# Fused LoRA-routed layer on one core: h transposed by transfers and VectorE instead of TensorE, a ring of four, tile 0 ordered by operand

## What is computed

```
logits = x @ Wr.T + 5.0 * one_hot(id, 8)
gates  = softmax of the two largest logits, scattered to their two experts, else 0
h      = (x @ A[e].T) for 8 experts of rank 16, each times its gate   (128 values per token)
cond   = x @ W.T + 2.0 * sum over experts of h[e] @ B[e].T
out    = x + softplus(scale) * (cond @ sign)
```

## Time and profile before

| | before |
|---|---|
| median of 3 runs, us | 165.47 (165.2 to 165.47) |
| the profiled execution's own time, us | 165.39 |
| its span, us | 163.6 |
| TensorE busy | 97% |
| VectorE, ScalarE, GpSimd busy | 59%, 40%, 32% |
| DMA, mean over the span | 119 GB/s |
| x loads, y stores: from issue to landing, us | 1.8, 2.1 |

### The profile page before, as it was taken

How to read it: one execution, slowest core, us unless ns; L and a number is a source line. 1 busy time by engine, 2 the same in 40 slices (tenths; PEclk the granted TensorE clock), 3 DMA queues, 4 the chain that set the end, 5 groups by cost and what they waited for, 6 DMA issues and landing times.

```text
span 163.6 us, 3711 instructions
## 1 busy us (share of the span) xinstructions
PE 159.1 (97%) x1070; PEld 154.3 (94%) x1070; DVE 96.5 (59%) x416; ACT 66.1 (40%) x177; POOL 51.7 (32%) x50
## 2 busy tenths in 40 slices
PE   7999989999999999999999999999999999999993
PEld 5788779999999999999999999999999999999992
DVE  5668995565566655555555555566655555455741
ACT  3653642434443333444443433443333444443340
POOL 2984435222223333333333222223333333333000
PEclk9999999999999999999999999999999999999999
...
GB/s 190 355 145 133 110 47 118 75 117 117 123 123 113 127 118 124 128 128 128 128 124 99 102 118 119 116 123 120 120 115 127 128 128 128 64 64 64 68 66 128
DMA packets 29431, 19.51 MB, mean 119 GB/s; under 512 B 7248, under 2 KB 24432, under 8 KB 29424
## 3 DMA queue, kind: packets, MB, share of 16 engines
...
HBM read 11.03 MB, written 8.39 MB: 119 GB/s over the span
## 4 chain that ended last, share of the span: by engine, by line
PE 94%; DVE 4%; ACT 1%; issue 0%
PE pair L643 69%; PE pair L663 14%; PE p_b L581 2%; PE p_ht L670 2%; PE pair L593 2%; PE pair L600 2%; PE pair L607 2%; DVE wide_lo L489 1%; DVE m_full L483 1%; PE pair L575 0%; PE pair L573 0%; PE pair L574 0%; ACT wide_hi L372 0%; DVE xt L435 0%; DVE wide_lo L475 0%; ACT y L398 0%
## 5 line engine op out<-in xcount | busy, mean ns | idle before, releaser
L300 POOL TENSOR_TENSOR xt_lo<-xt,xt_hi 128x512 fp32r<-128x512 f32 x32 | 41.2, 1288 | 91.1 <-ACT xt_hi L350 91.1
L643 PE MATMUL pair<-wide_hi,xt_hi 128*128 128x392 f32 (+1 forms) x256 | 63.0, 322 | 0.7 <-DVE wide_lo L489 0.6
L643 PE MATMUL pair<-wide_lo,xt_hi 128*128 128x392 f32 (+1 forms) x256 | 60.1, 311 | 0.0
L643 PE MATMUL pair<-wide_hi,xt_lo 128*128 128x392 f32 (+1 forms) x256 | 60.1, 311 | 0.0
L643 PEld LDWEIGHTS pair<-wide_hi,xt_hi 128*128 128x128 f32 x256 | 39.5, 189 | 1.6 <-DVE wide_lo L489 0.9
L643 PEld LDWEIGHTS pair<-wide_hi,xt_lo 128*128 128x128 f32 x256 | 39.8, 188 | 0.0
L643 PEld LDWEIGHTS pair<-wide_lo,xt_hi 128*128 128x128 f32 x256 | 39.8, 188 | 0.0
L397 ACT ACTIVATE y<-pair 128x256 f32<-128x256 f32 x31 | 11.9, 384 | 44.3 <-PE pair L663 44.3
L520 DVE TENSOR_TENSOR logits<-pair,bias 128x8 f32<-128x8 f32 x32 | 5.3, 166 | 37.0 <-PE pair L643 37.0
L435 DVE STREAM_TRANSPOSE xt<-x_in 128x512 f32<-128x512 f32 x32 | 22.7, 710 | 3.7 <-DVE top L528 3.2
L350 ACT ACTIVATE xt_hi<-xt 128x512 fp32r<-128x512 f32 x32 | 20.3, 633 | 2.1 <-DVE xt L435 2.1
...
## 6 DMA issues: line engine op xcount, KB each, us to landing
x_in<-in_x SPq DMA_DIRECT2D x128, 64.0 KB, 1.8
out<-y SPq DMA_DIRECT2D x31, 256.0 KB, 2.1
sign_in<-in_L_ffn_sign ACTq DMA_DIRECT2D x4, 256.0 KB, 5.2
w_in<-in_L_cond_W SPq DMA_DIRECT2D x4, 256.0 KB, 4.9
a_in<-in_L_cond_A SPq DMA_DIRECT2D x4, 64.0 KB, 5.1
b_in<-in_L_cond_B SPq DMA_DIRECT2D x4, 64.0 KB, 4.0
...
```

What stands on the lines that cost most here:

```text
L300: nc.gpsimd.tensor_tensor(xt_lo[n][:, :, :].rearrange("p j (g b) -> p g j b", g=NQ), xt[n][:, :, :, :], xt_hi[n][:, :, :].bitcast(FP32).re ...
L643: last = nc.tensor.matmul(pair[n][bank][:, at0:at0 + hi - lo], l[:, k, :], w[:, k, lo:hi], start=(opens and k == 0 and l is xt_hi[n] and w ...
```

## The change

- All rings have four buffers (RING), and LAG is three: `lora` in step s is for tile s - 3. The PSUM pairs take all eight banks; p_b2 is bank 0 of pair 3 (tile 3 waits for b2's low part), and p_ht is gone from the loop.
- h of tiles 0 to 28: SP issues four transfers from h_gated to h_moved (`move_h`), each of 32 columns from 128 partitions to 32 partitions in four rows, 128 bytes a piece. VectorE transposes h_moved in 32x32 blocks to ht in SBUF (`turn_h` on VectorE, right behind the logits), ScalarE makes ht_hi from it (`high_h`) and VectorE ht_lo, behind the maximum and ahead of x's transposition. ht_hi and ht_lo are written with a stride of four elements.
- h of tiles 29 to 31 is still transposed by TensorE (`turn_h(tile)` in `finish`), into banks of pairs that are free by then.
- Loads of x from tile 4 on: two of the four transfers are issued by SP, one tile of the ring ahead, and two by ScalarE (`load`), behind its xt_hi.
- `finish` is reordered: it now holds five groups of `lora`.
- Tile 0 (`first_tile`): all chunks of high-high first, then xt_lo times high, then high times wide_lo. b2's products with B's high part come first, then those with its low part.
- Written out in the prologue (not shown): ScalarE makes b_hi after the head's high parts, and xt_hi of tile 1 after all of M's high parts, with the four load issues for tiles 4 and 5 ahead of b2's high part. VectorE's order is fold 0, low parts of the head, b_lo, folds 1 to 3, transposition of x of tile 1, low parts of M's chunks 0, 2, 3 (before: b_lo, head, folds 0 and 1, transposition, low 0, folds 2 and 3, low 2 and 3). GpSimd makes xt_lo of tile 0 ahead of the bias.

The diff, without lines in which only S3 became RING and without the prologue's moved lines:

```diff
...
-h_gated = sb("h_gated", [P, ER])
+h_gated = [sb(f"h_gated{n}", [P, ER]) for n in range(RING)]
+h_moved = [sb(f"h_moved{n}", [P, NQ, Q]) for n in range(RING)]
+ht = sb("ht", [ER, NQ, Q])
...
 pair = [[ctx.enter_context(nc.psum_tensor(f"pair{n}{k}", [P, 512], FP32)) for k in range(2)]
-        for n in range(S3)]
-p_ht = ctx.enter_context(nc.psum_tensor("p_ht", [P, 512], FP32))
-p_b2 = ctx.enter_context(nc.psum_tensor("p_b2", [P, 512], FP32))
+        for n in range(RING)]
+p_b2 = pair[3][0]
 p_m = [pair[1][0], pair[1][1], pair[2][0], pair[2][1]]
+p_ht = {TILES - 3: pair[(TILES - 1) % RING][1], TILES - 2: pair[(TILES - 4) % RING][0],
+        TILES - 1: pair[(TILES - 4) % RING][1]}
...
+    return q + (r + d) // RING
 LEAD = 2
-LAG = 2
-FIRST = LAG + S3
...
+    def move_h(q, r, d):
+        n = slot(r, d)
+        sp_eng.wait_ge(h_gated_made, RING * q + r + d + 1)
+        for i in range(NQ):
+            sp_eng.dma_start(h_moved[n][Q * i:Q * i + Q, :, :], h_gated[n][:, Q * i:Q * i + Q])\
+                .then_inc(h_arrived[n], 16)
     def turnover(q, r, s):
-        if s is None or s + S3 < TILES:
-            sp_eng.wait_ge(xt_made, S3 * q + r + 1)
-            load(q, r, S3 * q + r + S3)
+        if s is None or 0 <= s - LEAD - 1 < LATE:
+            move_h(q, r, -LEAD - 1)
+        if s is None or s + RING < TILES:
+            sp_eng.wait_ge(xt_made, RING * q + r + 1)
...
+    def load(q, r, d):
+        n = slot(r, d)
+        act.wait_ge(xt_made, RING * q + r + d + 1 - RING)
+        for i in range(NQ // 2, NQ):
+            act.dma_start(x_in[n][Q * i:Q * i + Q, :, :], x_load[i, :, RING * q + r + d, :, :])\
+                .then_inc(x_loaded[n], 16)
+    high_x(0, 1, 0, first=True)
+    load(1, 0, 0)
+    load(1, 1, 0)
...
+    def high_h(done, late):
+        if late is None:
+            act.wait_ge(ht_made, done - LAG + 1)
+            nc.scalar.activation(ht_hi[:, :].rearrange("p (b g) -> p g b", g=NQ), ht[:, :, :], ACT.Copy)\
+                .then_inc(ht_hi_made, 1)
+        else:
+            act.wait_ge(ht_turned, late - LATE + 1)
+            act.wait_ge(y_summed, late)
+            nc.scalar.activation(ht_hi[:, :], p_ht[late][:, 0:P], ACT.Copy).then_inc(ht_hi_made, 1)
     def step(q, r, s):
-        if has(s, -LAG):
-            act.wait_ge(ht_turned, S3 * q + r - LAG + 1)
-            nc.scalar.activation(ht_hi[:, :], p_ht[:, 0:P], ACT.Copy).then_inc(ht_hi_made, 1)
+        if s is None or 0 <= s - LAG < LATE:
+            high_h(RING * q + r, None)
...
+        if s in (TILES - 1, TILES, TILES + 1):
+            high_h(s, s - 2)
...
         if has(s, LEAD):
-            high_x(q, r, LEAD, first=(s is not None and s + LEAD < S3))
+            high_x(q, r, LEAD, first=(s is not None and s + LEAD < RING))
+        if has(s, LEAD + RING):
+            load(q, r, LEAD + RING)
...
-    def low_h(done):
-        dve.wait_ge(ht_hi_made, done - LAG + 1)
-        nc.vector.tensor_tensor(ht_lo[:, :], p_ht[:, 0:P], ht_hi[:, :].bitcast(FP32), ALU.subtract)\
-            .then_inc(ht_lo_made, 1)
+    def low_h(done, late):
+        dve.wait_ge(ht_hi_made, done - LAG + 1 if late is None else late + 1)
+        if late is None:
+            nc.vector.tensor_tensor(ht_lo[:, :].rearrange("p (b g) -> p g b", g=NQ), ht[:, :, :],
+                                    ht_hi[:, :].bitcast(FP32).rearrange("p (b g) -> p g b", g=NQ),
+                                    ALU.subtract).then_inc(ht_lo_made, 1)
+        else:
+            nc.vector.tensor_tensor(ht_lo[:, :], p_ht[late][:, 0:P], ht_hi[:, :].bitcast(FP32),
+                                    ALU.subtract).then_inc(ht_lo_made, 1)
+    def turn_h(q, r, s):
+        n = slot(r, -LAG)
+        dve.wait_ge(h_arrived[n], 16 * NQ * (turn(q, r, -LAG) + 1))
+        nc.vector.transpose(ht[:, :, :].rearrange("p g b -> p (g b)"),
+                            h_moved[n][:, :, :].rearrange("p g c -> p (g c)")).then_inc(ht_made, 1)
     def step(q, r, s):
-        done = S3 * q + r
+        done = RING * q + r
         n = slot(r, -1)
         if has(s, -1):
...
                 .then_inc(logits_made, 1)
             dve.wait_ge(logits_made, done)
-        hurry = s is not None and s >= TILES - 1
-        if has(s, -LAG) and not hurry:
-            low_h(done)
+        if s is None or 0 <= s - LAG < LATE:
+            turn_h(q, r, s)
+        if s == TILES:
+            low_h(done, TILES - 3)
         if has(s, -1):
             nc.vector.max(top[:, :], logits[:, :]).then_inc(top_made, 1)
+        if s is None or 0 <= s - LAG < LATE:
+            low_h(done, None)
+        if has(s, -1):
             dve.wait_ge(top_made, done)
         if s == 0:
             turn_x(q, r, LEAD, first=True)
             low_b2()
         elif has(s, LEAD):
-            turn_x(q, r, LEAD, first=(s is not None and s + LEAD < S3))
+            turn_x(q, r, LEAD, first=(s is not None and s + LEAD < RING))
         if has(s, -1):
             nc.vector.max_index(top_at[:, :], top[:, :], logits[:, :]).then_inc(top_at_made, 1)
-        if has(s, -LAG) and hurry:
-            low_h(done)
         if has(s, -1):
             dve.wait_ge(top_at_made, done)
             nc.vector.tensor_copy(top_no[:, :], top_at[:, 0:2]).then_inc(top_no_made, 1)
...
+        if s == TILES + 1:
+            low_h(done, TILES - 1)
...
+    pe.wait_ge(b_hi_made, 1)
+    for j in range(OC):
+        for part in (sign_hi, sign_lo):
+            nc.tensor.matmul(p_b2[:, :], b_hi[:, j, :, :].rearrange("p e r -> p (e r)"), part[:, j, :],
+                             start=(j == 0 and part is sign_hi), stop=False, skip_group_check=True)
     pe.wait_ge(b_lo_made, 1)
     for j in range(OC):
-        last = three(p_b2[:, :], b_hi[:, j, :, :].rearrange("p e r -> p (e r)"),
-                     b_lo[:, j, :, :].rearrange("p e r -> p (e r)"),
-                     sign_hi[:, j, :], sign_lo[:, j, :], j == 0, j == OC - 1)
+        last = nc.tensor.matmul(p_b2[:, :], b_lo[:, j, :, :].rearrange("p e r -> p (e r)"), sign_hi[:, j, :],
+                                start=False, stop=(j == OC - 1), skip_group_check=True)
...
+    def first_tile():
+        for l, w in ((xt_hi[0], wide_hi), (xt_lo[0], wide_hi), (xt_hi[0], wide_lo)):
+            if w is wide_hi and l is xt_hi[0]:
+                pe.wait_ge(head_hi_made, 2)
+            elif w is wide_hi:
+                pe.wait_ge(xt_lo_made, 1)
             else:
-                pe.wait_ge(m_lo_made, (1, 0, 2, 3)[k])
+                pe.wait_ge(head_lo_made, 1)
+            for k in range(KC):
+                if w is wide_hi and l is xt_hi[0]:
+                    pe.wait_ge(m_hi_made, k + 1)
+                elif w is wide_lo and k == 1:
+                    pe.wait_ge(m_lo_second_made, 1)
+                elif w is wide_lo:
+                    pe.wait_ge(m_lo_made, (1, 0, 2, 3)[k])
+                for bank, lo, hi in BANKS:
+                    last = nc.tensor.matmul(pair[0][bank][:, 0:hi - lo], l[:, k, :], w[:, k, lo:hi],
+                                            start=(k == 0 and w is wide_hi and l is xt_hi[0]), stop=False,
+                                            skip_group_check=True)
+                    if w is wide_lo and k == KC - 1:
+                        last.then_inc((head_ready, wide_done)[bank], 1)
     def lora(n, banks):
...
-        pe.wait_ge(h_gated_made, done)
-        nc.tensor.transpose(p_ht[:, 0:P], h_gated[:, :], ident[:, :]).then_inc(ht_turned, 1)
+    def turn_h(tile):
+        pe.wait_ge(h_gated_made, tile + 1)
+        nc.tensor.transpose(p_ht[tile][:, 0:P], h_gated[tile % RING][:, :], ident[:, :]).then_inc(ht_turned, 1)
     def step(q, r, s):
-        done = S3 * q + r
-        if has(s, 0):
+        done = RING * q + r
+        if s == 0:
+            first_tile()
+        elif has(s, 0):
             pe.wait_ge(xt_lo_made, done + 1)
-            if s is None or s >= S3:
-                pe.wait_ge(y_copied, done - S3 + 1)
-            for k in range(KC // 2):
-                m_there(s, k)
-                wide(r, [k], BANKS, opens=True)
+            if s is None or s >= RING:
+                pe.wait_ge(y_copied, done - RING + 1)
+            if s == RING - 1:
+                pe.wait_ge(b2_lo_made, 1)
+            wide(r, range(KC // 2), BANKS, opens=True)
         if has(s, -LAG):
-            if s == LAG:
-                pe.wait_ge(b2_lo_made, 1)
             pe.wait_ge(ht_lo_made, done - LAG + 1)
             lora(slot(r, -LAG), (0, 1)).then_inc(y_summed, 1)
-        if has(s, 0):
-            for k in range(KC // 2, KC):
-                m_there(s, k)
-                wide(r, [k], BANKS, signals=True)
-        if has(s, -1):
-            turn_h(done)
+        if s != 0 and has(s, 0):
+            wide(r, range(KC // 2, KC), BANKS, signals=True)
     def finish(s):
-        before, r, n = (s - 1) % S3, s % S3, s % S3
+        before, r = (s - 1) % RING, s % RING
         first, second = range(KC // 2), range(KC // 2, KC)
```

(94 more changed lines are left out.)

80 lines of the change are left out of this document (37 added, 43 removed).

## The result

| | before | after |
|---|---|---|
| median, us | 165.33 (165.2 to 165.47, 4 runs) | 169.46 (167.77 to 169.75, 4 runs) |
| profiled execution, us | 165.39 | 169.75 |
| its span, us | 163.6 | 167.6 |
| chain that ended last | TensorE 94% | SyncE's queue 49%, TensorE 19% |

The ratio is 1.0215, 95% interval 1.0177 to 1.0254. The forecast was 162.1, faster by 2%: the wrong side.

A forecast was written before the change was run, and what follows sets the result against it. TensorE, without gaps in the loop, was taken as the bound. From 165.39, -3.19 (transposition), -1.34 (prologue) and +1.14 (finish) gave 162.0, forecast 162.1 with the median's 0.08; own range 161.5 to 162.8, full range 161.1 to 164.3.

The forecast's parts named there:

- SyncE's sum in part 2: Loop, SyncE's queue: four moves, two x loads and the store take 3.2 of a 4.27 us step, so in time.
- may be late by more than a step: Loop, SyncE: loads four tiles ahead and a store buffer needed four tiles later leave room for lateness.
- (a): Rival, loop: ScalarE's load issues delay the h matmuls; at 0.8 an issue 6.8 us more, 168.8; chance 0.09.
- (d): Rival, loop: moves land late and VectorE waits for h; 3.2 us lost again, 165.2; chance 0.05.
- the 0.10 given to "slower": Whole kernel: chance 0.10 of a slower result, made of (a) and a part of (d).
- The sign of being wrong: Loop: TensorE idle each step released by ht_lo, with ScalarE issues over 0.6 or VectorE waiting on h_arrived.
- b_in's 1.13 an issue: Upper bound for ScalarE's load issues, from four b_in issues taking 4.51; the likely value was 0.47 each.
- Tile 1 at 23.99, not 22.6: Prologue: tile 0 by operand removes gaps, -1.34 us, so tile 1 starts at about 22.6.
- 0.3 of slack: Loop's start: tile 0's moved h has two short steps of 3.56 ahead and about 0.3 us of slack.
- My own sentence on the exclusion of VectorE and GpSimd: Prologue: VectorE instructions with two SBUF inputs and GpSimd ones reading SBUF exclude each other; without it 0.2 us less.
- The forecast gaps of 0.49, 0.1, 0.3 and 0.25: Finish: TensorE waits before heads of tiles 31 and 28 and for h of tiles 30 and 31; together +1.14 us.
- The transposition's price: Loop: taking h's transposition off TensorE saves 0.11 in each of 29 tiles, -3.19 us; step 4.38 becomes 4.27.

The follow-up runs named there:

- run 5: The changed kernel with SyncE issuing one of each tile's four x loads and ScalarE three: 164.32 us, ratio 0.9916 to the kernel before.
- run 6: The changed kernel with SyncE issuing three of each tile's four x loads and ScalarE one: 180.0 us (one run).
- run 1: The changed kernel with no x load on SyncE in the loop, ScalarE issuing all four from tile 6 on: 164.55 us, ratio 0.9941 to before.
- run 2: The kernel before with only the change's prologue, transposition still on TensorE and lag two: 164.99 us, ratio 0.9976.
- run 7: The kernel before with four transfers of the move's shape added to each SyncE loop step, read by nobody: 188.58 us (one run).
- run 9 on the kernel before: run 2 with GpSimd waiting in step 1 for VectorE's gate of tile 0: 163.88 us, ratio 0.9894 to the kernel before.
- run 8: run 5 with own buffers for h parts of tiles 29 to 31, tile 31's transposition ahead of tile 30's h matmuls: 163.54 us, ratio 0.9883 to before.
- run 9 on run 8: run 8 with GpSimd waiting in step 1 for VectorE's gate of tile 0: 163.68 us, ratio 0.9881 to the kernel before.

## Why the prediction was wrong

**The step that failed** is SyncE's sum in part 2: "4 x 0.46 + 2 x 0.46 + 0.4 for the store, 3.2 of 4.27". It measured 4.46. Two terms were wrong. The move was priced by the x load's 0.46 from one issue to the next, and takes 0.60 with 0.04 behind it: four take 2.5, not 1.84, +0.66. And between the groups, where the waits and the address registers stand, 0.5 to 0.9 a step passes, 0.66 on the mean, which the sum put at nothing. The timeline of SyncE before shows such times already (0.36 and 0.18 here between the loads' end and the store, with no wait for y in this stretch), and I did not ask for it:

```profile
60.27 1.85 SPq L227 DMA_DIRECT2D x_in<-in_x  x4
62.48 0.37 SPq L233 DMA_DIRECT2D out<-y  x1
64.82 1.82 SPq L227 DMA_DIRECT2D x_in<-in_x  x4
66.82 0.37 SPq L233 DMA_DIRECT2D out<-y  x1
```

Either term alone would have left the sum at 3.8; with both the queue was over 4.27, and no slack in time ("may be late by more than a step") helps against a queue that is over the step in sum. No rival had SyncE: (a) put the danger on ScalarE, (d) on the landing, so the 0.10 given to "slower" stood on causes that did not come. The sign of being wrong did come, VectorE waiting for the moves and TensorE released by ht_lo, but I had meant it for late landings; the moves landed in 1.8 and were issued late. The part had a row for the landing's upper end and none for the issue's, though b_in's 1.13 an issue stood in it and was used for ScalarE alone. Four moves at that price would have been 4.5.

The Trainium skill, in "DMA: Bandwidth & Descriptors", section "Issuing engines are not separate DMA queues", says that issuing on several engines only saves the time on the sequencer, "which is usually small relative to the DMA itself". The first half agrees with runs 5 and 6: moving an issue changes the time only through SyncE's sequence, and the landings of moves, loads and stores stay at 1.9 to 2.2. The second half doesn't hold here: 0.60 to issue beside 1.8 to land, and with seven issues a tile the issue time was the kernel's bound.

**The sum, against the profiled execution.** Forecast 162.0, measured 169.75.
- Tile 1 at 23.99, not 22.6: +1.4. The order by operand works (one gap, 0.45, where I had 0.2), but W and sign landed late in this execution: ScalarE waited 1.82 for a part of W, and TensorE 1.32 for b_hi, which the change had put behind the head's parts. In runs 1 and 2 tile 1 started at 22.23 and 22.28, in run 5 at 23.00. Whether the new order makes a late W dearer wasn't tried.
- Tile 0's h parts: TensorE waits 0.94 for them, +0.9. I had 0.3 of slack; the gate of 1.29 took it. My own sentence on the exclusion of VectorE and GpSimd covered the low parts, not the gate.
- The steady steps, 26 from the first group of h matmuls at 33.86 to the one at 149.88: 26 x (4.46 - 4.27) = +5.0.
- The finish, from tile 30's first load to the end of the last: 12.27, I had 12.26, 0. The forecast gaps of 0.49, 0.1, 0.3 and 0.25 measured 0.60, 0, 0.25 and 0.19.
- From the last weight load to the end of the run 5.1, before 4.76: +0.35. It lies around the span: after and the six kernels built on it have 2.07 to 2.25 there, before and the four built on it 1.76 to 1.86, run 7 with its idle moves among them. So it isn't the moves' traffic; its cause is open.

Together +7.65, of 7.75.

**What held.** The transposition's price, in part: the step without SyncE's bound is 4.30, not 4.27; its 0.11 gave 0.08 back, -2.3 in place of -3.2. ScalarE's issues run beside its activations, as two issues of after at 71.48 and 71.97 do:

```profile
71.39 0.38 ACT L432 ACTIVATE y<-pair 128x256 f32<-128x256 f32 x1
71.48 0.33 ACTq L392 DMA_DIRECT2D x_in<-in_x  x1
71.66 0.63 ACT L364 ACTIVATE xt_hi<-xt 128x512 fp32r<-128x512 f32 x1
71.97 0.32 ACTq L392 DMA_DIRECT2D x_in<-in_x  x1
```

The landing (1.8, in runs 1 and 5 2.1; forecast 2.1) held. VectorE's transposition of h takes 0.31 (0.27), ht_hi 0.43 (0.28), ht_lo 0.39 (0.29): 0.29 more in a row than forecast, most of my slack of 0.35. In run 5 ht_lo ends only 0.1 to 0.2 before the load that needs it, not the 0.3 that I had named as a sign of being right, and TensorE never waits in the loop.

**Where the change's gain is.** The best kernel with the moves has 163.54, and the prologue with one more wait and the transposition still on TensorE 163.88. The ratios, 0.9883 and 0.9894, can't be told apart. So by the times nearly all of the 1.1% can be had from the prologue; most of what TensorE saves in the loop goes into tile 0's longer way, the finish and the 0.35 at the end. The traces leave a little for the moves: from tile 1's start to the end of the last weight load it is 136.7 in before and in run 9 on the kernel before, 135.9 in run 8 and 135.4 in run 9 on run 8, so 0.4 to 1.0 after the 0.35, from single executions.
